# A Mamba block and a mixture of experts on one core: the skip term goes into PSUM through ScalarE, the orders of all engines are rewritten, and the last expert is finished in halves

## The chip, the cores and the metric

The kernel runs on one core of one Trainium2 chip. The metric is the device time of one execution in microseconds (us); lower is better. Before the change the median of 3 runs is 1095.29 us (1094.91 to 1095.7). The five engines of the core run their own instruction queues in order and meet at semaphores: TensorE (PE), VectorE (DVE), ScalarE (ACT), GpSimd (POOL), and SyncE (SP), which issues nearly all DMAs.

## The reference

The input holds 32 sequences of 256 tokens with 128 channels. Two residual blocks follow each other:

```python
x = x + mamba(layernorm(x))
x = x + moe(layernorm(x))

# mamba: d_inner = 256, 16 states, 4 taps, rank 8
xi, res = split(x @ W_in)
u = silu(causal_conv(xi) + conv_b)
delta_r, B, C = split(u @ W_x)
delta = softplus(delta_r @ W_dt + b_dt)
h[t] = exp(delta * A) * h[t-1] + delta * B * u        # per channel and state
y[t] = sum over states of h[t] * C[t]
y = (y + u * D) * silu(res)                           # u * D is the skip term
out = y @ W_out
# moe: 8 experts, hidden 256, the two best of them weighted by a softmax
y = sum over e of cw[:, e] * (silu(x @ w1[e].T) @ w2[e].T)
```

## The kernel before, in words

The work is cut into 16 rounds of two sequences (512 tokens). In a round a tile of the recurrence holds 128 channels by 2 halves by 512 tokens, 128x1024 elements, and there are 16 of them, one for each state n. The names of the steps are those of the functions in the code. For each state n of round j:

- PE `row_b` (L1701) spreads the row of B over the partitions into the PSUM tile `rows`; it waits until the scan of state n-2 is done, since `rows` has two places.
- DVE `inputs` (L1224) multiplies it with `du` (delta * u), and DVE `scan` (L1235) runs the recurrence into a ring of 8 tiles `h`. ACT `decay` (L847) has written exp(delta * A) into `dA`.
- POOL `outputs` (L527) multiplies `h` with the row of C.
- PE `sum_states` (L1722) adds the tile to `y_ps`, two PSUM banks, by 8 transposes: `y_ps` is the sum over the states, turned so that tokens lie on the partitions.

When all 16 states are in, ACT `copy_y` (L860) copies `y_ps` to SBUF, PE `turn_y` (L1733) transposes it back into the two banks of `work` (banks 0 and 1), and DVE `gating` (L1266) multiplies both banks with silu(res). Then come PE `project_out`, DVE `residual` and `post_stats`, POOL `inverse_deviation` (the second layernorm), ACT `post_norm`, PE `turn_x2`, ACT `copy_x2T`, PE `score`, DVE `top_two`, the routing on POOL (`gap`, `routing`) with ACT `ratio_exp` between, and for each of the 8 experts twice PE `hidden` (L1770, into PSUM), twice ACT `hidden` (the silu, L883), PE `expert` (L1779), DVE `weight_expert` (L1303) and POOL `add_expert` (L569).

The skip term u * D goes in by ACT `skip` (L837), which writes it to the SBUF tile `ud`, and PE `skip_in` (L1710), 8 transposes that open the sum in `y_ps` ahead of the 16 states.

`work` has only two PSUM banks, which all of these steps share except the recurrence (`rows` takes four, `y_ps` two). Each PE step that writes a bank has a list of former users, and `free` waits for the first of them that exists. In the last three rounds, once `rows` comes free, the table `MOVED` puts hidden layers and experts into banks 2 to 5.

The order of the work is written out by hand for each engine. `round_(i)` is the steady body (a loop over pairs of rounds); ahead of it and behind it stand lists for the first and the last rounds. Five rounds are in flight at once: a body of PE, for example, holds the recurrence of round i-2, the experts of round i-4 and the front end of rounds i and i-1.

The end of the program is the last expert of round 15: 8 matmul pairs into one bank, one DVE `weight_expert`, one POOL `add_expert`, one DMA of 256 KB.

Of the kernel before, what the change touches and what calls it, by code (L numbers as in the profile page):

```python
# [17 lines left out]
H = 2  # L18
# [23 lines left out]
TURN_X2 = ("turn_x2", 1)  # L42
SCORE = ("score", 1)
HIDDEN = ("hidden", ((0, 1), (0, 1), (1, 0), (0, 0), (1, 0), (0, 1), (0, 0), (1, 0)))
# [5 lines left out]
MOVED = {("expert", 1, 0): 5, ("expert", 1, 1): 3, ("expert", 1, 2): 2, ("expert", 1, 4): 3, ("expert", 1, 5): 2,  # L50
         ("expert", 1, 6): 3, ("expert", 1, 7): 4, ("expert", 2, 0): 1, ("expert", 2, 1): 0, ("expert", 2, 2): 3,
         ("expert", 2, 3): 5, ("expert", 2, 4): 3, ("expert", 2, 5): 2, ("expert", 2, 6): 4, ("expert", 3, 1): 0,
         ("expert", 3, 2): 0, ("expert", 3, 4): 0, ("expert", 3, 5): 0, ("expert", 3, 7): 0,
         ("hidden", 1, 0, 1): 3, ("hidden", 1, 1, 0): 4, ("hidden", 1, 1, 1): 0, ("hidden", 1, 2, 0): 2,
         ("hidden", 1, 2, 1): 1, ("hidden", 1, 3, 0): 4, ("hidden", 1, 4, 1): 4, ("hidden", 1, 5, 0): 5,
         ("hidden", 1, 6, 0): 4, ("hidden", 1, 7, 0): 5, ("hidden", 1, 7, 1): 1, ("hidden", 2, 0, 0): 1,
         ("hidden", 2, 1, 1): 2, ("hidden", 2, 2, 0): 3, ("hidden", 2, 2, 1): 4, ("hidden", 2, 3, 0): 5,
         ("hidden", 2, 3, 1): 2, ("hidden", 2, 4, 0): 4, ("hidden", 2, 4, 1): 2, ("hidden", 2, 5, 0): 1,
         ("hidden", 2, 5, 1): 4, ("hidden", 2, 6, 0): 5, ("hidden", 2, 7, 0): 3, ("hidden", 2, 7, 1): 5,
         ("hidden", 3, 2, 1): 1, ("hidden", 3, 3, 0): 1, ("hidden", 3, 3, 1): 1, ("hidden", 3, 4, 1): 1,  # L60
         ("hidden", 3, 5, 0): 1, ("project_out", 1): 0, ("project_out", 2): 0, ("score", 1): 2}
# [30 lines left out]
def mamba_moe(nc, x, W_in, conv_w, conv_b, W_x, W_dt, b_dt, A_log, D, W_out, gate_wT, w1T, w2T, out):  # L92
# [27 lines left out]
    with ExitStack() as ctx:  # L120
# [50 lines left out]
        ud = sb("ud", [P, H, T])  # L171
# [79 lines left out]
        skip_summed = sem("skip_summed")  # L251
# [26 lines left out]
        expert_added = sem("expert_added")  # L278

# [29 lines left out]

        def two_seqs(ap):  # L310
            return ap.rearrange("p (s t) -> p s t", s=SEQS)
# [8 lines left out]
        def weigh_taps(half):  # L320

            at = slice(half * P, (half + 1) * P)
            nc.vector.tensor_tensor(w_conv[:, :, at], w_in[:, at].unsqueeze(1).broadcast_to([P, TAPS, P]),
                                 taps_rows.rearrange("p (d k) -> p k d", k=TAPS)[:, :, at],
                                 ALU.mult).then_inc(w_conv_ready, 1)

        @block.sync
        def _(sp):
# [23 lines left out]
            def store_out(j):  # L352
                if not there(j):
                    return
                sp.wait_ge(expert_added, j.count(E, E))
# [19 lines left out]
            def round_(i):  # L375
                three, four, five, seven = (i.later(-k) for k in (3, 4, 5, 7))
                load_again(five)
                load_c(four, 2)
                store_c(three)
                store_out(seven)  # L380
                load_c(four, 3)
                load_c(three, 0)
                load_c(three, 1)
                load_x(i)
# [25 lines left out]
            for g in range(CGROUPS):  # L410
                load_c(lead, g)
            load_again(r[0])
            load_again(r[1])
# [4 lines left out]
            load_c(r[1], 1)  # L418
            load_x(r[5])
            load_c(r[1], 2)  # L420
# [4 lines left out]
            load_c(r[2], 2)  # L425
            load_c(r[2], 3)
            store_c(r[3])
            load_c(r[3], 0)
            load_c(r[3], 1)
            load_x(r[6])  # L430
            run(sp, round_, 7, 7, 19)
            load_again(r[14])
# [7 lines left out]
            for odd in range(2):  # L440
                sp.wait_ge(out_stored[odd], 16 * (rounds // 2))

        @block.gpsimd
        def _(pool):
# [124 lines left out]
            def add_expert(j, e):  # L569
                if not there(j):  # L570
# [6 lines left out]
            def round_(i):  # L577
                two, three, four, five = (i.later(-k) for k in (2, 3, 4, 5))
                add_soft(two)
                times_u(two)  # L580
                add_expert(five, 4)
                outputs(three, 13)
                outputs(three, 14)
                add_expert(five, 5)
                gap(four)
                outputs(three, 15)
                outputs(two, 0)
                outputs(two, 1)
                outputs(two, 2)
                add_expert(five, 6)  # L590
                routing(four)
                add_expert(five, 7)
                outputs(two, 3)
                add_expert(four, 0)
                inverse_deviation(i, 0)
                outputs(two, 4)
                outputs(two, 5)
                add_expert(four, 1)
                outputs(two, 6)
                outputs(two, 7)  # L600
                outputs(two, 8)
                outputs(two, 9)
                add_expert(four, 2)
                outputs(two, 10)
                inverse_deviation(three, 1)
                add_expert(four, 3)
                outputs(two, 11)
                outputs(two, 12)

            inverse_deviation(r[1], 0)  # L610
            inverse_deviation(r[2], 0)
# [3 lines left out]
            outputs(r[0], 3)  # L615
            outputs(r[0], 4)
# [8 lines left out]
            inverse_deviation(r[4], 0)  # L625
# [1715 lines left out]
```

## Time and profile before

| | us |
|---|---|
| median of 3 runs | 1095.29 |
| the profiled execution's own time | 1093.58 |
| its span in the trace | 1091.6 |
| PE busy | 1039.5 (95%) |
| DVE busy | 1016.8 (93%) |
| POOL busy | 961.8 (88%) |
| ACT busy | 908.1 (83%) |

The span is the stretch from the first to the last recorded instruction; 1.98 us of the execution lie around it. "Busy" is the time in which an engine had at least one instruction under way. Matmuls overlap, so the mean of one matmul in a table is longer than its step in a chain; the steps of the chain of waits are what one of them costs when PE does nothing else. A weight (the share of the span) is a mean over a start, a long steady part and an end, which have different limits, so the stretches are read apart.

### The profile page before, as it was taken

What the parts mean: (1) busy time and instruction counts of PE and PEld (TensorE: products, weight loads), DVE (VectorE), ACT (ScalarE), POOL (GpSimd) and SP (SyncE); (2) the same over time, 40 slices, a digit from 0 to 9 for tenths busy, and PEclk for the clock granted to TensorE, in tenths of its full rate; (3) what the DMA queues carried; (4) which work ended last, traced back from release to release, by engine and by line L of the source; (5) the groups of instructions that cost most, each with busy time, mean ns of one, the idle gap of its engine ahead of it and who ended that gap; (6) DMA issues with size and microseconds to landing.
All of it is one profiled execution on the core that took longest, in us unless ns stands there. A gap on an engine that the chain in (4) does not pass through costs nothing.

```text
span 1091.6 us, 18705 instructions
## 1 busy us (share of the span) xinstructions
PE 1039.5 (95%) x6150; PEld 756.5 (69%) x6150; DVE 1016.8 (93%) x1054; ACT 908.1 (83%) x1379; POOL 961.8 (88%) x891
## 2 busy tenths in 40 slices
PE   7688779999999999999999999999999999989997
PEld 4446456677777767777777777767777776767775
DVE  5999999999999999999999999999999999999721
ACT  4987877989989998998989899899989989875533
POOL 4688986999999999999999999999999999799834
PEclk9798899999999999999999999999999999989999
DMA  5331212132040313104031311303130220320000
GB/s 201 138 127 57 78 60 79 59 117 69 6 167 14 127 59 122 63 30 153 2 126 58 126 58 64 120 0 130 54 136 39 88 87 0 137 87 11 11 10 11
DMA packets 37349, 84.12 MB, mean 77 GB/s; under 512 B 3305, under 2 KB 28193, under 8 KB 28961
## 3 DMA queue, kind: packets, MB, share of 16 engines
q1 hardware_dynamic: 36864, 83.06, 21.3%
q8 instruction: 25, 0.41, 0.2%
q14 instruction: 44, 0.35, 0.1%
q10 hardware_dynamic: 416, 0.30, 0.1%
HBM read 78.63 MB, written 4.72 MB: 76 GB/s over the span
## 4 chain that ended last, share of the span: by engine, by line
PE 82%; DVE 10%; issue 4%; ACT 3%; DMA 0%; POOL 0%; POOLq 0%; DVEq 0%; ACTq 0%
PE work L1786 19%; PE work L1776 18%; PE y_ps L1728 17%; PE work L1652 9%; DVE h L1241 6%; PE rows L1707 4%; PE work L1749 2%; PE work L1636 2%; PE work L1671 2%; PE rows L1786 2%; PE work L1662 2%; DVE rows L1231 2%; PE rows L1776 1%; PE work L1697 1%; PE y_ps L1717 1%
## 5 line engine op out<-in xcount | busy, mean ns | idle before, releaser
L534 POOL TENSOR_TENSOR h<-h,c_rows 128x1024 f32<-128x1024 f32 x256 | 600.4, 2368 | 52.2 <-DVE h L1241 52.1
L1241 DVE TENSOR_TENSOR_SCAN h<-dA,rows 128x1024 f32<-128x1024 f32 x256 | 579.4, 2277 | 1.1
L855 ACT ACTIVATE dA<-delta,a_neg 128x510 f32<-128x510 f32 x512 | 326.2, 709 | 8.0 <-DVE h L1241 4.6
L1231 DVE TENSOR_TENSOR rows<-du,rows 128x1024 f32<-128x1024 f32 x256 | 306.8, 1215 | 3.9 <-PE rows L1707 3.7
L1728 PEld LDWEIGHTS y_ps<-ident,h 128*128 128x128 f32 x2048 | 241.3, 144 | 61.5 <-issue 33.5
L1728 PE MATMUL y_ps<-ident,h 128*128 128x128 f32 x2048 | 270.0, 278 | 10.7 <-POOL h L534 10.7
L1786 PEld LDWEIGHTS work<-w,hid 128*128 128x128 f32 x1856 | 223.2, 193 | 35.1 <-ACT hid L889 18.9
L1776 PE MATMUL work<-x2T,w 128*128 128x512 f32 x474 | 238.5, 598 | 3.4 <-ACT u L773 2.8
L1786 PE MATMUL work<-w,hid 128*128 128x128 f32 x1856 | 229.1, 277 | 2.7 <-ACT hid L889 2.2
L889 ACT ACTIVATE hid<-work 128x512 f32<-128x512 f32 x237 | 139.4, 596 | 64.0 <-PE work L1776 62.2
L574 POOL TENSOR_TENSOR x<-x,weighted 128x512 f32<-128x512 f32 x128 | 163.6, 1278 | 21.6 <-DVE weighted L1310 21.1
L1776 PEld LDWEIGHTS work<-x2T,w 128*128 128x128 f32 x474 | 81.7, 190 | 57.3 <-issue 19.5
L1707 PE MATMUL rows<-parts,select 96*128 96x512 bf16 x256 | 100.3, 392 | 21.1 <-DVE h L1241 19.7
L1652 PE MATMUL work<-xnT,w_conv 128*128 128x512 f32 x256 | 116.3, 597 | 0.5 <-ACT xnT L765 0.5
L739 ACT ACT_TABLE_LOAD x74 | 94.9, 1283 | 1.3
L889 ACT ACT_TABLE_LOAD x56 | 71.8, 1283 | 20.5 <-PE work L1776 14.7
L1310 DVE TENSOR_TENSOR weighted<-work,cw 128x512 f32<-128x512 f32 x116 | 78.6, 677 | 8.6 <-PE work L1786 6.8
L1652 PEld LDWEIGHTS work<-xnT,w_conv 128*128 128x128 f32 x256 | 47.4, 191 | 49.0 <-issue 47.9
L1707 PEld LDWEIGHTS rows<-parts,select 96*128 96x128 bf16 x256 | 25.4, 100 | 56.7 <-DVE h L1241 28.5
L1310 DVE TENSOR_TENSOR weighted<-rows,cw 128x512 f32<-128x512 f32 x12 | 8.2, 691 | 32.3 <-PE rows L1786 20.5
L525 POOL TENSOR_TENSOR du<-delta,u 128x1024 f32<-128x1024 f32 x15 | 35.4, 2363 | 1.8 <-POOL delta L518 1.3
L518 POOL TENSOR_TENSOR delta<-du,soft 128x1024 f32<-128x1024 f32 x15 | 35.4, 2361 | 0.0
(141 smaller groups left out, 954.3 us busy)
## 6 DMA issues: line engine op xcount, KB each, us to landing
c_rows<-c_dram SPq DMA_DIRECT2D x64, 1024.0 KB, 4.8
x_in<-in_x SPq DMA_DIRECT2D x16, 256.0 KB, 2.9
x_again<-in_x SPq DMA_DIRECT2D x16, 256.0 KB, 3.4
out<-x SPq DMA_DIRECT2D x16, 256.0 KB, 2.6
w<-in_w1T SPq DMA_DIRECT2D x1, 1024.0 KB, 4.9
w<-in_w2T SPq DMA_DIRECT2D x1, 1024.0 KB, 7.1
h<-in_conv_w SPq DMA_DIRECT2D x1, 512.0 KB, 4.8
c_dram<-bcd SPq DMA_DIRECT2D x16, 32.0 KB, 1.6
```

What stands on the lines that cost most here:

```text
L534: nc.gpsimd.tensor_tensor(at, at, c_rows[:, n, :].unsqueeze(1).broadcast_to([P, H, T]), ALU.mult).then_inc(c_used, 1)
L574: nc.gpsimd.tensor_tensor(x1[:, j.odd], x1[:, j.odd], weighted[:, e % 2], ALU.add).then_inc(expert_added, 1)
L739: nc.scalar.preload_act_table_set("natural_log_exp_and_others")
L855: last = nc.scalar.activation(two_seqs(dA[:, n % RING, half, :])[:, :, 1:], two_seqs(delta[:, half, :])[:, :, 1:], ACT.Exp, scale=a_neg[:, ...
L889: nc.scalar.activation(hid[:, e % 2, f, :], bank(place(HIDDEN, j, e, f)), ACT.Silu).then_inc(hid_ready, 1)
L1231: nc.vector.tensor_tensor(rows[:, n % 2], du[:, j.odd], rows[:, n % 2, H - 1, :].unsqueeze(1).broadcast_to([P, H, T]), ALU.mult).then_inc( ...
L1241: nc.vector.tensor_tensor_scan(h[:, n % RING].rearrange("p h t -> p (h t)"), dA[:, n % RING].rearrange("p h t -> p (h t)"), rows[:, n % 2] ...
L1652: last = nc.tensor.matmul(two_seqs(work[:, CONV[half], :]), w_conv[:, k, half * P:(half + 1) * P], xnT[:, :, k:k + SEQ], start=(k == 0), s ...
L1707: nc.tensor.matmul(rows[:, n % 2, H - 1, :], select[:, n, :], parts[:, j.odd, :], start=True, stop=True).then_inc(b_ready, 1)
L1728: last = nc.tensor.matmul(y_ps[:, half, b, :], h[:, n % RING, half, b * P:(b + 1) * P], ident[:, :], is_transpose=True, start=False, stop= ...
L1776: nc.tensor.matmul(bank(place(HIDDEN, j, e, f)), w1[:, e, f, :], x2T[:, j.odd, :], start=True, stop=True).then_inc(hid_projected, 1)
L1786: last = nc.tensor.matmul(token_bank(place(EXPERT, j, e))[:, b, :], hid[:, e % 2, f, b * P:(b + 1) * P], w2[:, f, e, :], start=(f == 0), s ...
```

## The change

- `skip` becomes one step for each half, and writes u * D straight into bank 0 or 1 of `work` (ACT, SBUF to PSUM). `turn_y` adds onto it: its transposes no longer open the bank. `skip_in`, the tile `ud` and the semaphore `skip_summed` are gone, and the first `sum_states` of a round opens `y_ps`. `skip` waits for the former users of its bank, as PE's steps do.
- The matmuls of `expert` and `project_out` open a bank once instead of once for each block of 128 tokens.
- The last expert of round 15 runs through its first hidden half for all tokens and then the second, into two banks; DVE adds cw times the expert to x1 in four 128x128 steps, without POOL, and each half is stored by a DMA of its own.
- The orders of all engines, the table of banks `HIDDEN` and `MOVED` are new. The steady body of PE starts at another step; POOL, DVE and SP issue `add_soft`, the stats of the next layernorms and the loads at other places.

```diff
-            def skip(j):
+            def skip(j, half, *uses):
                 if not there(j):
                     return
                 act.wait_ge(u_ready, j.count(H, H))
-                wait(act, skip_summed, j.count(1, 0))
-                for half in range(H):
-                    last = nc.scalar.activation(ud[:, half, :], u[:, j.odd, half, :], ACT.Copy,
-                                                scale=skip_w[:, half:half + 1])
-                last.then_inc(skip_ready, 1)
+                free(act, *uses)
+                nc.scalar.activation(bank(TURN_Y[half]), u[:, j.odd, half, :], ACT.Copy,
+                                     scale=skip_w[:, half:half + 1]).then_inc(skip_ready, 1)
...
-            def skip_in(j):
...
-                for half in range(H):
-                    for b in range(TB):
-                        last = nc.tensor.matmul(y_ps[:, half, b, :], ud[:, half, b * P:(b + 1) * P], ident[:, :],
-                                                is_transpose=True, start=(b == 0), stop=False,
-                                                skip_group_check=True)
-                last.then_inc(skip_summed, 1)
...
             def sum_states(j, n):
                 if not there(j):
                     return
                 pe.wait_ge(c_used, j.count(NS, n + 1))
+                if n == 0:
+                    wait(pe, yT_ready, j.count(1, 0))
...
-            def turn_y(j, half, *uses):
+            def turn_y(j, half):
                 if not there(j):
                     return
                 pe.wait_ge(yT_ready, j.count(1, 1))
-                free(*uses)
-                turn(work[:, TURN_Y[half], :], yT[:, half], y_turned)
+                pe.wait_ge(skip_ready, j.count(H, half + 1))
+                turn(work[:, TURN_Y[half], :], yT[:, half], y_turned, onto=True)
...
+                if is_last(j, e):
+                    pe.wait_ge(yT_ready, rounds)
+                    for f in range(FH):
+                        pe.wait_ge(hid_ready, j.count(E * FH, FH * e + f + 1))
+                        for b in range(TB):
+                            half, first = b // (TB // 2), b % (TB // 2) == 0
+                            last = nc.tensor.matmul(last_half_bank(half)[:, b, :], hid[:, e % 2, f, b * P:(b + 1) * P],
+                                                    w2[:, f, e, :], start=(first and f == 0),
+                                                    stop=(not first and f == FH - 1), skip_group_check=True)
+                            if f == FH - 1 and not first:
+                                last.then_inc((last_half_done, expert_done)[half], 1)
+                    return
...
-MOVED = {("expert", 1, 0): 5, ("expert", 1, 1): 3, ("expert", 1, 2): 2, ("expert", 1, 4): 3, ("expert", 1, 5): 2,
+MOVED = {("expert", 1, 0): 1, ("expert", 1, 1): 5, ("expert", 1, 2): 2, ("expert", 1, 3): 5, ("expert", 1, 4): 2,
...
```

The first place is on PE in the steady body, around the two `turn_y` of a round (`work<-ident,yT`). `y_ps<-ident,h` is `sum_states`, `rows<-parts,select` is `row_b`, `work<-x2T,w1` is a `hidden`, `work<-w2,hid` an `expert`. Before:

```order
L1776 MATMUL work<-x2T,w1 128x512
L1631 REGISTER_ALU
L1776 MATMUL work<-x2T,w1 128x512
L1717 MATMUL y_ps<-ident,ud 128x128 x8
L1631 REGISTER_ALU
L1636 MATMUL work<-ident,yT 128x128 x4
L1631 REGISTER_ALU
L1636 MATMUL work<-ident,yT 128x128 x4
L1728 MATMUL y_ps<-ident,h 128x128 x24
L106 REGISTER_ALU
L1707 MATMUL rows<-parts,select 128x512
L1786 MATMUL work<-w2,hid 128x128 x8
```

And now:

```order
L1874 MATMUL work<-x2T,w1 128x512
L105 REGISTER_ALU
L1814 MATMUL rows<-parts,select 128x512
L1825 MATMUL y_ps<-ident,h 128x128 x8
L1834 REGISTER_ALU
L1742 MATMUL work<-ident,yT 128x128 x8
L105 REGISTER_ALU
L1814 MATMUL rows<-parts,select 128x512
L1825 MATMUL y_ps<-ident,h 128x128 x8
L1897 MATMUL work<-w2,hid 128x128 x8
```

The 8 transposes of `ud` are gone, a `row_b` and one `sum_states` stand ahead of the turn in their place, and one `sum_states` with a `row_b` instead of three is left between the turn and the expert.

The second place is on ACT in the steady body, behind `copy_y` (`yT<-y_ps`), with the silu of two hidden halves and then the skip into `work`:

```order
L950 ACTIVATE yT<-y_ps 128x1024
L105 REGISTER_ALU
L973 REGISTER_ALU
L974 ACTIVATE hid<-work 128x512
L973 REGISTER_ALU
L974 ACTIVATE hid<-work 128x512
L929 ACTIVATE work<-u,skip_w 128x512 x2
L825 ACT_TABLE_LOAD
```

Before, the two skips stood about half a round earlier, between `copy_xnT` and the last hidden layers, and nothing on this path waited for them.

The third place is on PE at the end of the program, from the second-last `sum_states` of round 15 on. Before:

```order
L1728 MATMUL y_ps<-ident,h 128x128 x8
L1786 MATMUL work<-w2,hid 128x128 x8
L1728 MATMUL y_ps<-ident,h 128x128 x8
L1776 MATMUL rows<-x2T,w1 128x512 x2
L1636 MATMUL work<-ident,yT 128x128 x4
L1776 MATMUL rows<-x2T,w1 128x512
L1636 MATMUL work<-ident,yT 128x128 x4
L1786 MATMUL rows<-w2,hid 128x128 x8
```

And now:

```order
L1825 MATMUL y_ps<-ident,h 128x128 x16
L1874 MATMUL work<-x2T,w1 128x512
L1897 MATMUL rows<-w2,hid 128x128 x8
L1874 MATMUL rows<-x2T,w1 128x512
L1825 MATMUL y_ps<-ident,h 128x128 x8
L1897 MATMUL rows<-w2,hid 128x128 x8
L1742 MATMUL work<-ident,yT 128x128 x4
L1874 MATMUL rows<-x2T,w1 128x512
```

Before, the experts of round 14 behind the last `sum_states` begin with its third; now they begin with its fourth, and three hidden halves more stand ahead of it. From the last `sum_states` to the end PE has 27 `hidden`, 14 `expert` before and 24 and 13 now.

## Rows read from the trace of the kernel before

**Rows 1.** The page, its first part: busy time and share of the span.

```profile
PE 1039.5 (95%) x6150; PEld 756.5 (69%) x6150; DVE 1016.8 (93%) x1054; ACT 908.1 (83%) x1379; POOL 961.8 (88%) x891
```

**Rows 2.** Two stretches: length, busy PE, PEld, DVE, ACT, POOL, clock, DMA share, GB/s.

```profile
200.00:900.00 700.00, 698.02 (x4242) 514.16 (x4241) 693.05 (x718) 639.67 (x966) 665.04 (x598) 1.00 0.22 79
...
31.50:1028.60 997.10, 959.11 (x5723) 700.79 (x5724) 983.41 (x976) 869.57 (x1314) 921.90 (x807) 0.98 0.21 76
```

**Rows 3.** Groups of instructions, 200 to 900 us: busy us, mean ns, idle before.

```profile
L1241 DVE TENSOR_TENSOR_SCAN h<-dA,rows 128x1024 f32<-128x1024 f32 x178 | 403.5, 2278 | 0.8
...
L739 ACT ACT_TABLE_LOAD x56 | 71.8, 1283 | 1.0
...
L843 ACT ACTIVATE ud<-u,skip_w 128x512 f32<-128x512 f32 x22 | 14.6, 720 | 0.0
...
L1717 PE MATMUL y_ps<-ident,ud 128*128 128x128 f32 x88 | 11.4, 273 | 0.0
```

**Rows 4.** Timeline of DVE: start, length, instruction, idle time ahead of it.

```profile
99.68 1.23 DVE L1272 TENSOR_TENSOR yT<-work,gate 128x1024 f32<-128x1024 f32 x1 [1.21 <-PE work L1636]
...
133.00 2.36 DVE L1231 TENSOR_TENSOR rows<-du,rows 128x1024 f32<-128x1024 f32 x2 [2.06 <-PE rows L1707]
...
554.91 0.69 DVE L1281 TENSOR_TENSOR x<-x_again,work 128x512 f32<-128x512 f32 x1 [0.31 <-PE work L1749]
...
977.57 1.23 DVE L1231 TENSOR_TENSOR rows<-du,rows 128x1024 f32<-128x1024 f32 x1 [0.88 <-PE rows L1707]
```

**Rows 5.** Chain of waits near the end: start, length, engine, line.

```profile
991.56 0.22 PE rows L1707
991.78 0.88 PE y_ps L1728 x8
992.66 0.86 PE work L1776 x2
993.52 1.78 PE work L1786 x16
```

**Rows 6.** Timeline of ACT, PE and DVE around one steady gating.

```profile
534.52 1.03 ACT L865 ACTIVATE yT<-y_ps 128x1024 f32<-128x1024 f32 x1
...
536.28 0.60 ACT L889 ACTIVATE hid<-work 128x512 f32<-128x512 f32 x1 [0.24 <-PE work L1776]
...
536.02 1.04 PE L1717 MATMUL y_ps<-ident,ud 128*128 128x128 f32 x8
...
538.13 1.20 DVE L1272 TENSOR_TENSOR yT<-work,gate 128x1024 f32<-128x1024 f32 x1
```

**Rows 7.** Stretches of 4 us, columns as in rows 2.

```profile
228.00:232.00 4.00, 2.96 (x20) 2.45 (x20) 3.01 (x4) 3.96 (x6) 3.47 (x12) 1.00 0.00 0
...
960.00:964.00 4.00, 2.54 (x22) 2.31 (x20) 3.90 (x15) 3.99 (x7) 4.00 (x3) 1.00 0.01 2
964.00:968.00 4.00, 2.02 (x9) 1.33 (x9) 4.00 (x3) 4.00 (x7) 4.00 (x3) 0.70 0.00 2
968.00:972.00 4.00, 3.72 (x17) 3.68 (x18) 3.96 (x4) 1.59 (x5) 4.00 (x4) 0.50 0.00 0
```

**Rows 8.** Timeline of the end, all engines.

```profile
1025.11 1.21 DVE L1231 TENSOR_TENSOR rows<-du,rows 128x1024 f32<-128x1024 f32 x1
1026.35 2.29 DVE L1241 TENSOR_TENSOR_SCAN h<-dA,rows 128x1024 f32<-128x1024 f32 x1
...
1084.06 0.60 ACT L889 ACTIVATE hid<-work 128x512 f32<-128x512 f32 x1 [2.20 <-PE work L1776]
...
1084.71 2.05 PE L1786 MATMUL rows<-w,hid 128*128 128x128 f32 x16 [0.75 <-ACT hid L889]
1086.80 0.69 DVE L1310 TENSOR_TENSOR weighted<-rows,cw 128x512 f32<-128x512 f32 x1 [2.97 <-PE rows L1786]
1087.57 1.26 POOL L574 TENSOR_TENSOR x<-x,weighted 128x512 f32<-128x512 f32 x1 [2.39 <-DVE weighted L1310]
1088.86 0.37 SPq L356 DMA_DIRECT2D out<-x  x1
```

More of the change, by code:

```diff
@@ L1848, in round_ @@
-                row_b(two, 12)
-                hidden(four, 5, 0, use_expert(four, 3))
-                sum_states(two, 9)
-                hidden(four, 5, 1, use_expert(four, 4))
-                row_b(two, 13)
                 hidden(four, 6, 0, use_hid(four, 5, 0))
@@ L1868, in round_ @@
[L1868 to L1869 removed]
+                expert(four, 6, use_xnT(i), use_x2T(three), use_hid(four, 6, 1))
                 sum_states(two, 12)
[L1871 to L1873 removed]
+                sum_states(two, 13)
+                row_b(one, 1)
+                expert(four, 7, use_scores(three), use_hid(four, 7, 1))
@@ new lines, in round_ @@
+                sum_states(two, 14)
+                row_b(one, 2)
+                hidden(three, 0, 0, use_expert(four, 6), use_xnT(i), use_x2T(three))
+                hidden(three, 0, 1, use_expert(four, 7), use_scores(three))
+                sum_states(two, 15)
+                hidden(three, 1, 0, use_hid(three, 0, 0))
+                hidden(three, 1, 1, use_hid(three, 0, 1))
+                row_b(one, 3)
+                sum_states(one, 0)
+                turn_y(two, 0)
+                turn_y(two, 1)
@@ L1905, in round_ @@
[L1905 to L1915 removed]
+                         use_hid(four, 2, 0), use_u(one, 0))
@@ new lines, in round_ @@
+                row_b(one, 5)
+                convolve(i, 1, use_expert(three, 0), use_gated(two), use_hid(three, 1, 0), use_hid(three, 0, 0),
+                         use_expert(four, 6), use_xnT(i))
+                row_b(one, 6)
+                hidden(three, 2, 0, use_u(i, 0), use_gated(two), use_hid(three, 1, 1))
+                row_b(one, 7)
+                hidden(three, 2, 1, use_u(i, 1), use_expert(three, 0))
+                expert(three, 1, use_hid(three, 2, 0))
+                project_bcd(i, use_hid(three, 2, 1), use_u(i, 1))
@@ L1916, in round_ @@
+                sum_states(one, 2)
+                row_b(one, 8)
                 expert(three, 2, use_expert(three, 1))
+                take_high(i)
+                row_b(one, 9)
                 sum_states(one, 3)
-                take_high(i)
+                take_middle(i)
+                project_out(two, use_expert(three, 2), use_expert(three, 1), use_hid(three, 2, 0), use_u(i, 0),
+                            use_gated(two))
+                hidden(three, 3, 0, use_low(i), use_hid(three, 2, 1))
@@ L1919, in round_ @@
                 sum_states(one, 4)
-                row_b(one, 8)
-                take_middle(i)
+                project_gate(i, 0, use_x1(two), use_expert(three, 2), use_expert(three, 1), use_hid(three, 2, 0),
+                             use_u(i, 0))
+                row_b(one, 10)
+                delta_rank(i, 0, use_hid(three, 3, 0), use_low(i))
+                sum_states(one, 5)
+                project_gate(i, 1, use_gate(i, 0))
+                hidden(three, 3, 1, use_dt(i, 0), use_hid(three, 3, 0))
@@ L1923, in lead_in @@
+                row_b(one, 11)
+                hidden(three, 4, 0, use_gate(i, 1), use_gate(i, 0), use_x1(two), use_expert(three, 2))
+                hidden(three, 4, 1, use_hid(three, 3, 1))
+                sum_states(one, 6)
             def lead_in():
@@ L2209, in _ @@
+            turn_y(r[14], 1)
+            row_b(r[15], 4)
             expert(r[13], 0, use_gated(r[14]))
             hidden(r[13], 2, 0, use_gated(r[14]))
+            row_b(r[15], 5)
+            expert(r[13], 1, use_expert(r[13], 0))
+            sum_states(r[15], 1)
+            sum_states(r[15], 2)
+            project_out(r[14], use_expert(r[13], 1))
             row_b(r[15], 6)
-            expert(r[13], 1, use_expert(r[13], 0))
-            sum_states(r[15], 2)
+            hidden(r[13], 2, 1, use_hid(r[13], 2, 0))
```

1110 lines of the change are left out of this document (526 added, 584 removed).

## The prediction

> **What bounds the kernel now.** I read the shares first, and they don't decide it: PE 95%, DVE 93%, POOL 88% [rows 1]. So I read the steady part alone, 200 to 900 us. There PE is busy 698.0 of 700 us, DVE 693.1, POOL 665.0, ACT 639.7 [rows 2]. It holds 178 scans [rows 3], and 16 make a round, so a round takes 700 / 178 x 16 = 62.9 us; in it PE is busy 62.7 us and DVE 62.3. The reader is to see that two engines are full at once: what is taken from PE alone can shorten a round by 0.6 us at most, and less where DVE's gaps are the spacing of its own dependent instructions.
>
> The timeline of DVE shows which gaps are waits. A steady round has one, of about 0.3 us, for `project_out` ahead of `residual` [rows 4], the third row there; I count 12 rounds at that. In the first rounds DVE waits 1.21 and 2.06 us, near the end 0.88 us [rows 4], with a few smaller ones between. From the first scan to the last, DVE is busy 983.4 of 997.1 us [rows 2]: 13.7 us of gaps, of which I read some 10 as waits.
>
> Behind the last scan, which ends at 1026.35 + 2.29 = 1028.64 [rows 8], DVE has little to do. There PE alone sets the end with what is left of the experts of rounds 14 and 15, and then come one DVE, one POOL step and a store. This tail is 1091.6 - 1028.6 = 63.0 us.
>
> The sum is thus: when does the last scan end, and how long is the tail.
>
> **PE's work.** The chain of waits gives the prices while PE is full: 0.88 us for 8 transposes, 0.86 for a `hidden`, 1.78 for an `expert` [rows 5]. `skip_in` is 8 transposes, once in each of 16 rounds: 16 x 0.88 = 14 us leave PE (by its busy time, 11.4 us over 11 rounds [rows 3], it is 16.6). That is the most the change can take by this route.
>
> **The end of the last scan.** DVE's own instructions stay the same but for two small things. One `weight_expert` of round 14 now stands ahead of the last scan instead of behind it, +0.6 us. And four fewer `inputs` are followed at once by their own scan, each worth about 0.12 us (a scan right behind its own `inputs` starts 1.24 us after it [rows 8], while the second of two `inputs`, which take 2.36 together [rows 4], starts 1.12 after the first), -0.5. What can go is the waits, 10 us at most. In a steady round PE now needs 62.7 - 0.9 = 61.8 us against DVE's 62.3 to 62.6, so `project_out` is in time and 0.3 us a round should go, 3.6 in 12 rounds; of the early and late waits, some 6 us, PE's smaller load should take a good third, 2.2. Against this stands a new wait.
>
> **The new wait.** Before, `turn_y` needed only `copy_y` and free banks, and three `sum_states` (2.6 us) lay between it and the next user of bank 0, an `expert`, which waits for the gating. Now the path from the last `hidden` of the four goes: silu 0.6, skip 0.7 and 0.7 (0.72 each into SBUF [rows 3]), turn of the second half 0.44, gating. With `copy_y` at 534.5 [rows 6] ACT would be through with both silus at 536.6 and with both skips at 538.0, the turn at 538.5; before, the gating started at 538.13 with no wait [rows 6]. What queues behind a late gating on DVE is everything: the next `inputs` and the scans. DVE's new order puts the gating behind `inputs` 3 instead of behind scan 3, so it comes there 3 us earlier relative to the scans; PE, which now has slack, is earlier as well. I make it -0.7 to +0.5 us of wait a round, and take 0.15, 1.8 us in 12 rounds. PE itself will wait at the next `expert`: it has 0.22 + 0.88 us of work there [rows 5] where it had 2.9, and the gating takes 1.2, so about 1.2 us, and some 0.5 at a `row_b`. That is 1.7 us a round against a slack of 0.5 to 0.8. It still fits where PE works ahead of DVE: walked through with the prices above, the later `row_b` of the round come 0.4 to 1.6 us before DVE asks for them.
>
> The skip's price in PSUM no row shows. A 128x512 ACT copy without a scale out of PSUM is 0.60, the skip into SBUF 0.72; I bound it by 0.5 and 1.2 and take 0.7. By 1.2 the gating would be 1 us late in every round, 12 us: that is part of the slow rival. The Trainium skill ("ScalarE: Activation LUTs", step-by-step section) says that PSUM is the faster destination for ScalarE; no row here shows it, and by it the skip would fall below 0.72 and the new wait towards nothing.
>
> ACT also loads its tables less often: 8 switches a round in the new order against 10, 2 x 1.28 us [rows 3]. ACT is busy 57.5 of 62.9 us [rows 2] and DVE waits for it nowhere in the steady part, so this is worth nothing in itself; it pays for the skip being in a worse place. POOL (59.8 us busy a round) keeps its instructions. Walked through, its new order starts the steady `outputs` close behind the scans and is just in time for `sum_states`; I cost it at 0, with 0.5 a round as the bound. The DMAs are the same, and their engines are busy 22% [rows 2].
>
> So the last scan: 1028.6 + 0.6 - 0.5 - 3.6 - 2.2 + 1.8 = 1024.7.
>
> **The tail.** Behind the last `sum_states` PE has 3 `hidden` and 1 `expert` less: 3 x 0.86 + 1.78 = 4.4 us. The path behind that sum (copy, turn, gating, projection, residual, stats, deviation, norm, turn, copy) has 15.8 us of round 14's steps as cover (5 `expert`, 8 `hidden`), where it had 20.1 and PE waited for none of it. What other engines do on it is `copy_y` 1.03 and gating 1.20 [rows 6], and after the projection four short steps on DVE, POOL and ACT, together some 10 us by my estimate. So the cover holds and I take 4.3.
>
> At the very end, the last silu is done at 1084.66 and the store is issued at 1088.86, 4.2 us [rows 8]: 2.05 for the expert, 0.69 DVE, 1.26 POOL and their spacing. Now the first half of the matmuls runs before that silu, 0.9 us remain, with 0.2 of delay, then two DVE steps of 128x128 for the last half. No row has that form; 128x512 takes 0.69, so a pair lies between 0.35 and 0.9 and I take 0.6. With spacing 1.8 against 4.2: -2.4, between 1.5 and 2.7. The store's own end I leave as it is. Tail: 63.0 - 4.3 - 2.4 = 56.3.
>
> **Sum.** Span 1024.7 + 56.3 = 1081.0, 10.6 us less than 1091.6. The profiled execution took 1093.58, so 1083.0 for a like one; the median of the runs is 1.7 us above that execution, hence 1084.7. Changes within 0.2% (2.2 us) can't be told from none.
>
> **Rivals.**
>
> *PE was the only true bound (0.15).* PE's busy share of 99.7% speaks for it; DVE's 99.0% with gaps of 0.04 to 0.1 us speaks against. Then all 14 us go, and the 2.4 at the end: 1095.3 - 16.4 = 1079.
>
> *The gating eats the steady gain (0.20).* The skip makes it 0.3 to 0.5 us late in each round, as the ACT times above allow, and the early waits come back in other places. Then the last scan ends where it did, or 2 us later, and only the tail is left, 6.7 us: 1089 to 1091.
>
> *PE loses its clock in the steady part (slower, 0.09).* At 960 to 968 us PE was busy only 2.54 and 2.02 of 4 us, and behind it the granted clock fell to 0.50, half of 2.4 GHz; in 228 to 232, with 2.96 of 4, it stayed at 1.00 [rows 7]. At half clock 4 us of work need 8, so such a fall costs PE 2 to 3 us. The new order has two PE waits close together around the turn in each round, 1.7 us. If they come to 3 us, from a skip nearer to 1.2 or a late POOL, the clock falls there in every second round: 6 x (2.5 + 1.3 - 0.5) = 20 us, less 6.7: 1109. It decides against the change from about 1.1 us of net loss a round on. The Trainium skill ("TensorE: Matmul & The Clock Gate", section on psum-queue depth-cycling) says that cycling through PSUM banks can leave PE idle often and briefly enough for the clock to swing; by that rule the banks held from skip to gating would do this here. The trace agrees only in that a fall follows idle PE time; around the steady turns of the kernel before, the clock stays at 1.00.
>
> *It comes out even (0.06).* POOL half a microsecond late in each round, and a routing in the tail that comes after the experts it weights: 1093 to 1097.
>
> The forecast has 0.50, from 1081 to 1088. Faster by over 0.2%: 0.50 + 0.15 + 0.18 = 0.83; within 0.2%: 0.08; slower: 0.09. The range runs from below the first rival to the even case, 1077 to 1094.
>
> **What the new profile would show.** Right: no L1717-like transposes of `ud`; a steady round of 62.5 to 62.8 us, DVE above 99.2% busy, PE at 97%, and its idle time released by DVE's gating and scans; the last scan at 1023 to 1027; 55 to 58 us from there to the end; no POOL step behind the last expert. Wrong: DVE waiting for `work<-ident,yT` in each round (the second rival); a clock below 1.00 between 300 and 900 us (the third); DVE still above 62.8 a round with no waits at all, which would say that its work, not its waits, was underpriced; PE idle in the tail for cw or for the norm, which would say that the cover of round 14 was too thin.

## The result, and the profile of the changed kernel

The changed kernel takes 1123.81 us (median of 4 runs, 1121.13 to 1125.44) against 1095.1 for the kernel before (4 runs, 1092.95 to 1095.7). The ratio is 1.026, with a 95% interval from 1.025 to 1.028: 2.6% slower, where I had forecast 1084.7. The profiled execution took 1121.13 us, with a span of 1119.3.

The first part of the page of the changed kernel, as [rows 1]:

```profile
PE 1043.6 (93%) x6022; PEld 746.1 (67%) x6022; DVE 1018.3 (91%) x1057; ACT 889.7 (79%) x1361; POOL 960.2 (86%) x890
```

The busy times hardly differ from those of before (PE 4.1 us more, with 128 matmuls fewer; DVE 1.5 more; ACT 18 and POOL 1.6 less), and all are smaller shares of a longer span. The stretch from 200 to 900 us, with the columns of [rows 2]:

```profile
200.00:900.00 700.00, 671.71 (x3975) 485.54 (x3973) 665.70 (x681) 591.36 (x905) 637.05 (x575) 1.00 0.22 80
```

The holes in this stretch have grown: PE 28 us where it had 2, DVE 34 where it had 7, POOL 63 where it had 35. The granted clock is 1.00 over the stretch as a whole. The groups of that stretch, as [rows 3]:

```profile
L591 POOL TENSOR_TENSOR h<-h,c_rows 128x1024 f32<-128x1024 f32 x172 | 404.1, 2366 | 40.6 <-DMA c_rows<-c_dram 33.2 <-DVE h L1340 7.3
L1340 DVE TENSOR_TENSOR_SCAN h<-dA,rows 128x1024 f32<-128x1024 f32 x170 | 383.2, 2275 | 0.7
...
L929 ACT ACTIVATE work<-u,skip_w 128x512 f32<-128x512 f32 x22 | 14.2, 684 | 0.0
```

170 scans where there were 178: 700 / 170 x 16 = 65.9 us a round against 62.9. The skip into PSUM takes 684 ns, a little less than the 720 into SBUF. The new thing stands behind the first row: POOL's `outputs` waits for a DMA, `c_rows<-c_dram`, which loads the rows of C spread over the partitions. The waits in that stretch, longest first (engine, tile, line, what it waits for: us in total, times, longest), for POOL, PE and DVE:

```profile
POOL h L591 <- DMA c_rows<-c_dram: 33.2, 8, 4.6
...
PE y_ps L1825 <- POOL h L591: 23.3, 26, 1.3
...
DVE rows L1330 <- PE rows L1814: 16.3, 13, 2.5
...
DVE weighted L1422 <- POOL x L631: 9.2, 8, 1.2
```

The chain is plain: eight waits of 4.2 us, and two more at the same place (3.6 and 3.8 us, of the 7.3 that the view puts down to DVE), so ten in the ten rounds between 205 and 800 us; then PE's `sum_states` behind POOL, then DVE behind PE's `row_b`, and DVE is the engine that a round is made of. One such place on POOL (timeline, columns as in [rows 4]):

```profile
529.45 2.38 POOL L591 TENSOR_TENSOR h<-h,c_rows 128x1024 f32<-128x1024 f32 x1
535.99 7.01 POOL L591 TENSOR_TENSOR h<-h,c_rows 128x1024 f32<-128x1024 f32 x3 [4.16 <-DMA c_rows<-c_dram]
```

The DMA queue of SP around it (start, time on the sequencer, the transfer):

```profile
491.05 0.40 SPq L413 DMA_DIRECT2D out<-x  x1
526.88 0.39 SPq L390 DMA_DIRECT2D x_in<-in_x  x1
527.57 0.38 SPq L400 DMA_DIRECT2D x_again<-in_x  x1
528.06 0.44 SPq L429 DMA_DIRECT2D c_rows<-c_dram  x1
528.61 0.36 SPq L419 DMA_DIRECT2D c_dram<-bcd  x1
536.00 1.28 SPq L429 DMA_DIRECT2D c_rows<-c_dram  x3
```

`c_rows` comes in four groups of four states a round (1 MB each). The one at 528.06 is the last group of the round that POOL is in; POOL would have taken it up at 529.45 + 2.38 = 531.83. It was issued at 528.06 and landed at 535.99, 7.9 us later. It stands behind `x_in`, which SP may only issue once ACT's `pre_norm` has read the old one:

```profile
524.97 1.64 ACT L834 ACTIVATE xn<-x_in,shift,rstd 128x128 f32<-128x128 f32 x4
```

That ends at 526.61, and `x_in` goes out at 526.88. The issue ahead of it is the store of `out` at 491.05, so the queue stood for 36 us at `load_x`, and everything behind it with it. In the same place of the kernel before, the order was another:

```profile
510.60 0.39 SPq L340 DMA_DIRECT2D x_in<-in_x  x1
511.19 0.39 SPq L350 DMA_DIRECT2D x_again<-in_x  x1
512.61 0.34 SPq L372 DMA_DIRECT2D c_rows<-c_dram  x1
...
551.35 7.98 SPq L372 DMA_DIRECT2D c_rows<-c_dram  x3
```

There the `c_rows` at 512.61 is the third group, and the fourth is the first of the three from 551.35 on, ahead of the next `x_in`. In the code, the steady body of SP read `store_out(seven), load_c(four, 3), load_c(three, 0), load_c(three, 1), load_x(i)`; the changed one reads `store_out(seven), load_x(i), load_again(four), load_c(four, 3), store_c(three)`. The last load of C has been moved behind two loads of x. The page's list of DMAs shows it too, by the median time from issue to landing (KB each, us), after:

```profile
c_rows<-c_dram SPq DMA_DIRECT2D x64, 1024.0 KB, 6.7
...
c_dram<-bcd SPq DMA_DIRECT2D x16, 32.0 KB, 7.1
```

and before:

```profile
c_rows<-c_dram SPq DMA_DIRECT2D x64, 1024.0 KB, 4.8
...
c_dram<-bcd SPq DMA_DIRECT2D x16, 32.0 KB, 1.6
```

The number, size and bytes of these transfers are the same. Only what stands ahead of each is not.

Behind two of the ten waits, at 540 and 738 us, the granted clock falls too. Stretches of 4 us around the first, columns of [rows 2]:

```profile
532.00:536.00 4.00, 4.00 (x36) 3.80 (x35) 4.00 (x3) 3.59 (x5) 0.01 (x1) 1.00 0.37 139
536.00:540.00 4.00, 2.38 (x20) 1.95 (x18) 3.90 (x17) 4.00 (x8) 4.00 (x2) 1.00 0.79 272
540.00:544.00 4.00, 3.27 (x15) 3.12 (x16) 1.45 (x2) 1.82 (x5) 4.00 (x4) 0.57 1.02 428
```

POOL stands first (0.01 busy of 4), then PE (2.38), and only then is the clock at 0.57, near the lower of its two levels; DVE is hit last (1.45). The two rounds with such a fall take 67.1 and 66.9 us from gating to gating, the six others between 289 and 817 us 65.7 at the mean, so the clock makes up less than 3 us of the loss, and it comes behind POOL's wait.

### The profile page after: what moved, and what is told of

Read it like the earlier page. It is cut to its first block, busy times and chain, and to the rows that moved or that the text cites. A ratio compares the mean times of both kernels' runs of the same rounds, so it can differ in the third digit from the quotient of the medians.

```text
span 1119.3 us, 18572 instructions
## 1 busy us (share of the span) xinstructions
PE 1043.6 (93%) x6022; PEld 746.1 (67%) x6022; DVE 1018.3 (91%) x1057; ACT 889.7 (79%) x1361; POOL 960.2 (86%) x890
## 4 chain that ended last, share of the span: by engine, by line
PE 40%; DVE 26%; issue 20%; POOL 11%; ACT 2%; DVEq 1%; DMA 0%; POOLq 0%; ACTq 0%
DVE h L1340 13%; PE work L1897 8%; DVE rows L1330 8%; POOL h L591 8%; PE work L1874 8%; PE y_ps L1825 7%; PE work L1759 6%; PE rows L1897 2%; PE rows L1814 2%; POOL x L631 2%; DVE weighted L1422 2%; PE work L1742 1%; PE rows L1874 1%; PE work L1769 1%; PE work L1778 1%
## 5 line engine op out<-in xcount | busy, mean ns | idle before, releaser
L1825 PE MATMUL y_ps<-ident,h 128*128 128x128 f32 x2048 | 279.8, 282 | 32.7 <-POOL h L591 31.3
L1769 PE MATMUL work<-xnT,w_in 128*128 128x512 f32 x64 | 35.0, 630 | 0.2 <-DVE weighted L1422 0.2
```

The source lines that it names most:

```text
L1825: last = nc.tensor.matmul(y_ps[:, half, b, :], h[:, n % RING, half, b * P:(b + 1) * P], ident[:, :], is_transpose=True, start=(n == 0 and ...
```

## The experiments

The leading theory, L: the place of `load_c(four, 3)` in SP's order is the whole loss, and what is left of the change is about what I forecast. Its rivals: the skip's way through PSUM or the new orders of PE, ACT and POOL cost the time and the late DMA only shows up beside it; or the new end costs.

**1. The changed kernel with the load of C first.**

```diff
                 load_c(four, 2)
+                load_c(four, 3)
                 store_out(seven)
                 load_x(i)
                 load_again(four)
-                load_c(four, 3)
                 store_c(three)
```

and likewise, ahead of `load_x`, at two places of the list for the first rounds. The load also passes `store_out` here; as the rows above show, that store was issued 36 us before `x_in`, so it isn't what held the load.

> The changed kernel, with one edit on SP: the load of the last four C rows of a round (load_c group 3) stands ahead of store_out and of load_x, in the steady body and in the two places of the start; nothing else moves. Theory L (the loss sits in this queue: load_x waits for the pre_norm two rounds on, the C rows queue behind it, and POOL stands 4.2 us in each round until they land): POOL's waits for c_rows go from 33 us to below 3, a steady round from 66.1 to 62.5-63.0 us, and the time from 1123 to 1083-1093. Rival S (the loss is the skip that holds banks 0 and 1: turn and gating late, PE and then DVE behind it): POOL would only wait for something else, the time stays above 1112. Rival P (POOL's new order has no slack left): 1095-1110, with POOL at 95% busy and DVE waiting for row_b as now.

Measured: 1088.98 us (4 runs, 1087.64 to 1090.84); ratio to the kernel before 0.995 (0.994 to 0.997). That is 35 us below the changed kernel. The two groups that had waited:

```profile
L591 POOL TENSOR_TENSOR h<-h,c_rows 128x1024 f32<-128x1024 f32 x180 | 422.6, 2368 | 0.5 <-DVE h L1340 0.4
L1340 DVE TENSOR_TENSOR_SCAN h<-dA,rows 128x1024 f32<-128x1024 f32 x178 | 401.4, 2277 | 0.7
```

POOL's 40.6 us of idle time ahead of `outputs` are 0.5. The first half of L holds, and this kernel is faster than both, by 0.5% against the kernel before. The second half doesn't: what is left of the change is 5.4 us (1094.41 - 1088.98, the kernel before in the same set of runs), half of the 10.6 that I had forecast.

**2. The kernel before with the load of C late.** The move alone, in the old code:

```diff
                 store_out(seven)
-                load_c(four, 3)
                 load_c(three, 0)
                 load_c(three, 1)
                 load_x(i)
+                load_c(four, 3)
```

> The kernel before, with the reverse edit on SP alone: in the steady body the load of the last four C rows stands behind load_x, as in the changed kernel. Theory L: POOL's multiply of state 12 has to wait for a load that is issued only after the pre_norm two rounds on; the load would be issued about 574.3 in the round where POOL wants it about 575.6, and needs 6 to 8 us to land, so POOL stands 4 to 6 us a round; 3 to 5 us of it reach the round: 1095 to 1130-1155. Rivals S and P: the queue is innocent and the time stays within 5 us of 1095.

Measured: 1130.57 us (4 runs, 1127.09 to 1135.46), ratio 1.033 (1.030 to 1.036). Its waits, 200 to 900 us:

```profile
POOL h L534 <- DMA c_rows<-c_dram: 42.1, 9, 6.1
DVE rows L1231 <- POOL du L525: 37.6, 9, 5.6
```

The same wait, of 4.7 us at the mean, and the same size of loss, with nothing else of the change in it. It reaches DVE by another road, `du`, which stands behind the waiting `outputs` on POOL. With 1 this shows the cause from both sides. One thing differs from the changed kernel: only `x_in` stands directly ahead of the load, not both loads of x. The load is issued at 529.08, and POOL would have taken it up at 530.53, 1.5 us later; in the changed kernel POOL comes 3.8 us after the issue. So the size of the wait hangs on when `pre_norm` lets the queue go as much as on what stands ahead.

**3. The load of C between the two loads of x,** to tell which part of the path makes it late: the wait of `load_x` for `pre_norm`, or the transfer of `x_again` in front.

```diff
                 load_x(i)
-                load_again(four)
                 load_c(four, 3)
+                load_again(four)
```

> The changed kernel; on SP, in the steady body, the load of the last four C rows stays behind load_x but goes ahead of load_again, so that only the 256 KB of x_in, not both loads of x, are ahead of it. It tells how much of POOL's 4.2 us a round is the wait of the queue for pre_norm and how much is the transfers in front. Theory L: the load is issued about 0.5 us sooner after x_in (its place after load_again was 528.06, load_x 526.88) and shares the engines with 256 KB less (about 1 us): POOL's wait falls from 4.2 to 2.5-3.5 us a round, the time from 1123 to 1107-1118. If it were all wait for pre_norm, at least 1119; if all transfers, below 1100.

Measured: 1097.38 us (10 runs, 1092.96 to 1101.9), ratio 1.003 (1.002 to 1.005). I expected more, 1107 to 1118, and had set below 1100 as the sign that the transfers ahead make the whole wait: one place in the queue is worth 26 of the 35 us. The waits of POOL and DVE, 200 to 900 us:

```profile
POOL h L591 <- DMA c_rows<-c_dram: 15.4, 10, 3.7
...
DVE weighted L1422 <- POOL x L631: 2.6, 3, 1.2
```

The wait is 1.5 us a round at the mean where it was 4.1 over the ten rounds, and DVE hardly feels it: 2.6 us behind POOL's `x`. Two rounds side by side show what the place is worth. In both POOL comes 5.2 us after the end of `pre_norm`. In the changed kernel the load is issued 1.45 us after that end and lands 7.9 us later, so POOL waits 4.2; here it is issued 0.8 us after it and lands 5.4 us later, so POOL waits 1.0. Of the 3.2 us, 0.7 are the earlier issue and 2.5 the shorter landing behind `x_in` alone. Neither reason makes the wait by itself: the stop at `pre_norm` leaves only those 5.2 us, which a landing of 4.8 just fits and one behind other transfers doesn't.

POOL's slack swallows a wait of that size. The span of the profiled execution is 1091.3, 4.3 us above that of experiment 1, and counted by the scans 4.0 of it has arisen by the end of the seventh round, where the waits are 1.7 to 3.7 us; in the rounds behind, the waits are 0.6 to 1.1 us and a round takes 62.8 as in experiment 1. That execution (1093.14) is at the fast end of the ten, so the median has a larger loss that this trace doesn't show.

The Trainium skill ("DMA: Bandwidth & Descriptors", section on queues, rings and completion order) says that on each DMA engine the descriptors of one issuing engine's queue are consumed in the order of its ring. The traces agree: a 32 KB store behind 1.5 MB of loads took 7.1 us to land (median) and 1.6 before.

**4. The kernel before with the new end only** (the last expert by halves, DVE adds, two stores):

```diff
+                    for f in range(FH):
+                        pe.wait_ge(hid_ready, j.count(E * FH, FH * e + f + 1))
+                        for b in range(TB):
+                            half, first = b // (TB // 2), b % (TB // 2) == 0
+                            last = nc.tensor.matmul(last_half_bank(half)[:, b, :], hid[:, e % 2, f, b * P:(b + 1) * P],
```

> The kernel before with the new end alone: the last expert by halves into two banks, four 128x128 steps on DVE that add it to x1, no POOL step, two stores. By the prediction's sum -2.4 us (1.5 to 2.7), so 1092.4 to 1093.8. If the two DVE steps of a half cost more than 0.9 us, or the second store takes as long as the whole one did and adds its own start, the gain is below 1 us.

Measured: 1091.27 us (8 runs, 1090.24 to 1093.01), ratio 0.997 (0.996 to 0.998), 3.1 us less where I had expected 2.4. From the end of the last silu to the store:

```profile
1084.43 0.60 ACT L904 ACTIVATE hid<-work 128x512 f32<-128x512 f32 x1 [2.20 <-PE work L1804]
...
1085.91 0.61 DVE L1330 SCALAR_TENSOR_TENSOR x<-rows,cw,x 128x128 f32<-128x128 f32 x2 [1.71 <-PE rows L1819]
1086.44 0.60 DVE L1330 SCALAR_TENSOR_TENSOR x<-y_ps,cw,x 128x128 f32<-128x128 f32 x2
```

The silu is done at 1085.03, DVE at 1087.04: 2.0 us, where silu to store was 4.2 [rows 8]. A pair of the new DVE steps takes 0.60, as taken. From the end of the last silu to the end of the span it is 4.4 us here and 6.9 in the kernel before, 2.6 less.

**5. The kernel before without `skip_in`.** The skip term is left out of the sum; ACT still computes it. This gives the most that taking 8 transposes from PE can bring in the old order.

```diff
-                skip_in(one)
...
-                                                ident[:, :], is_transpose=True, start=False, stop=(n == NS - 1),
+                                                ident[:, :], is_transpose=True, start=(n == 0 and b == 0), stop=(n == NS - 1),
```

> The kernel before without skip_in: the skip term is left out of the sum (ScalarE still makes it, nobody reads it), and the first sum_states opens the bank. Orders untouched, so PE loses 0.88 us in each of 16 rounds and nothing else changes. It tells what PE's relief is worth by itself. If DVE's own work bounds the round (a_c3_first stands at 62.77 us a round with hardly a wait, before at 62.98), a round goes from 62.98 to 62.65-62.8 and the kernel gains 2 to 5 us: 1090-1093. If PE was the bound, it gains 12 to 14 us: 1080-1083.

Measured: 1090.1 us (4 runs, 1088.93 to 1091.62), ratio 0.996 (0.994 to 0.997), 3.7 us less. So of 16 x 0.88 = 14 us of PE work, 3.7 are felt. DVE's timeline has two gatings, six rounds apart:

```profile
410.99 1.20 DVE L1271 TENSOR_TENSOR yT<-work,gate 128x1024 f32<-128x1024 f32 x1
...
787.57 1.20 DVE L1271 TENSOR_TENSOR yT<-work,gate 128x1024 f32<-128x1024 f32 x1
```

376.58 / 6 = 62.76 us a round. And of experiment 1:

```profile
409.38 1.23 DVE L1371 TENSOR_TENSOR yT<-work,gate 128x1024 f32<-128x1024 f32 x1
...
786.02 1.23 DVE L1371 TENSOR_TENSOR yT<-work,gate 128x1024 f32<-128x1024 f32 x1
```

376.64 / 6 = 62.77. A round with the skip in PSUM is as short as one with no skip at all, against 62.98 in the kernel before, whose gatings start at 412.16 and 790.03, 377.87 / 6. So in the steady rounds the gain is whole, and small: DVE sets it. That is the steady part alone, and the two kernels differ in all their orders; the last scan of this one starts at 1023.25, 2.1 us ahead of that of experiment 1.

**6. Experiment 1 with the skip undone:** ACT writes `ud` again and PE's `skip_in` adds it, in the new orders. ACT's `skip` moves too, from behind the silus to ahead of the first `decay` of the round.

```diff
-            def skip(j, half, *uses):
+            def skip(j):
...
+            def skip_in(j):
+                pe.wait_ge(skip_ready, j.count(1, 1))
```

> The changed kernel with the same SP edit as a_c3_first, and the skip undone: ScalarE writes u*D to SBUF ahead of the first decay of the round, PE opens y_ps with 8 transposes of it ahead of the first sum_states, turn_y opens its banks and waits for their former users; the orders are otherwise those of the change. Against a_c3_first: if the skip through PSUM takes 0.88 us of PE a round and costs a gating wait of some 0.3 us, a_c3_first is 0 to 6 us faster; rival S says that this kernel is the faster one, by 5 us or more; if DVE alone bounds the round, the two are within 3 us.

Measured: 1129.27 us (4 runs, 1128.02 to 1131.12), ratio 1.033 (1.031 to 1.034), 40 us above experiment 1. A clear miss. Its gatings:

```profile
413.39 1.23 DVE L1360 TENSOR_TENSOR yT<-work,gate 128x1024 f32<-128x1024 f32 x1 [1.39 <-PE work L1731]
482.96 1.23 DVE L1360 TENSOR_TENSOR yT<-work,gate 128x1024 f32<-128x1024 f32 x1 [1.39 <-PE work L1731]
547.15 1.23 DVE L1360 TENSOR_TENSOR yT<-work,gate 128x1024 f32<-128x1024 f32 x1 [1.39 <-PE work L1731]
```

Rounds of 69.6 and 64.2 us take turns. The 64.2 is 62.8 plus the wait of 1.39 in each round. Two things now stand on the path to `turn_y`: `skip_in`, 0.87 us, and ACT, which with its `skip` at the earlier place brings two silus 1.2 us later against the scans, so that PE waits for it:

```profile
PE work L1873 <- ACT hid L977: 9.7, 12, 0.9
```

The 5.4 us more in every second round look like this on PE:

```profile
580.15 0.60 PE L1793 MATMUL work<-parts,w_dt 96*128 96x512 bf16 x2 [1.85 <-issue]
580.59 0.61 PE L1896 MATMUL work<-w,hid 128*128 128x128 f32 x4
583.10 2.72 PE L1896 MATMUL work<-w,hid 128*128 128x128 f32 x12 [1.90 <-issue]
```

"issue" is time in which PE waited for nothing that the profile shows, once in the middle of an `expert`, whose 16 matmuls need nothing new after the fourth. The granted clock falls behind it to 0.75 and 0.50, and DVE waits 4.95 us for a `row_b`. The body of the loop holds two rounds, so both stops come once in each pass. The page's list of queues has a row that goes with it, here:

```profile
q8 instruction: 61, 1.00, 0.4%
```

(packets, MB, share). The packets are 25 in the kernel before, 24 in experiments 1 and 5, and 61 here. The trace has their times, too. In experiment 1 there is none between 422 and 946 us, while PE goes round its loop (until 941), and in the kernel before none between 411 and 935. Here nine of 16 KB come in each pass of the loop, and in the pass that begins at 576.3 the first three start at 577.3, 580.6 and 584.4, around the two stops (578.3 to 580.1 and 581.2 to 583.1). So here the loop is loaded anew in each pass, and in the others it isn't. That PE waits in the two stops for its instructions is still an inference, from these times, the place and the period; the profile names no releaser.

**7. The same with two waits fewer in PE's loop,** to see whether the loop was one or two instructions too long for something.

```diff
-                pe.wait_ge(yT_ready, j.count(1, 1))
+                if half == 0:
+                    pe.wait_ge(yT_ready, j.count(1, 1))
```

> a_c3_pe_skip (1129.3) with two wait instructions fewer in PE's loop: turn_y of the second half doesn't repeat its wait for copy_y. In a_c3_pe_skip every second round took 69.6 us against 64.2: PE stood twice 1.9 us with nothing that it waited for, the granted clock fell behind it, and the page counts 61 packets of instruction loads on a queue that has 24 or 25 in all other kernels; PE's loop has one instruction more than that of the kernel before. Theory I (PE's loop is just too long to be kept, and part of it is fetched anew in each pass): 24-25 packets, all rounds 64.2 us, 1098-1108 in all, and against a_c3_first (1089) that is what the skip on PE costs in this order, through a gating 1.4 us late. Rival: the stall is a wait that the profile doesn't show, for a bank or for ACT, and the time stays at 1124-1132.

Measured: 1125.36 us (4 runs, 1122.43 to 1128.22), ratio 1.027 (1.025 to 1.029). The packets are still 61 and both stops are there. I had expected 1098 to 1108 if the loop was too long. The waits turned out to ride on instructions that remain: a pass of the loop has 1,643 records on PE in both traces, so this says nothing on length. The kernel before has 1,637 in a pass and no such stop, the changed kernel 1,613. A limit between 1,637 and 1,643 isn't ruled out, and where the loop lies wasn't varied. This stays open. It also means that experiment 6 doesn't price the skip's move; 5 beside 1 does so for the steady rounds alone.

## Why the prediction was wrong, step by step

**The step that failed: "The DMAs are the same, and their engines are busy 22%".** With it went POOL's "I cost it at 0, with 0.5 a round as the bound". The DMAs are the same in number and bytes; their order in SP's queue is not, and a mean share of 22% says nothing on when one transfer lands. I read PE, ACT, POOL and DVE place by place and never SP. The price could have been worked out: the diff moves `load_c(four, 3)` behind `load_x`, whose issue waits for `pre_norm`, so its time is the start of `pre_norm` plus its length plus two issues plus a landing of at least 4.8 us behind 512 KB, against the fourth group's use on POOL. Measured, it lands 4.2 us late in each round. About 1 us of that POOL absorbs and 3.2 remain (66.0 us a round, from gatings at 420.26 and 684.39 four rounds apart, against 62.77). With ten such rounds that makes the 32 us by which the last scan is later than in experiment 1 (1057.64 against 1025.36):

```profile
1057.64 2.27 DVE L1340 TENSOR_TENSOR_SCAN h<-dA,rows 128x1024 f32<-128x1024 f32 x1
```

```profile
1025.36 2.27 DVE L1340 TENSOR_TENSOR_SCAN h<-dA,rows 128x1024 f32<-128x1024 f32 x1
```

(the changed kernel, then experiment 1). Behind it both take the same: 1119.3 - 1059.9 = 59.4 and 1087.0 - 1027.6 = 59.4. So of the error of 39 us, 35 are this step (1123.8 - 1089.0), and 4 come from the terms below, which experiment 1 lets me read one by one. (On the spans they are 6.0, 1087.0 against 1081.0; I had added 1.7 to come from one execution to the median, which that kernel doesn't need.)

**The last scan: forecast 1024.7, in experiment 1 1027.6, 1.0 us earlier than before.** The steady waits: 3.6 less 1.8 for the new gating wait, so 1.8 net; measured 62.98 - 62.77 = 0.21 a round, 2.5 in 12, so the net was nearly right. Its two terms weren't: the waits for `project_out` are 1.9 us in all in the kernel before, not 3.6, and the steady gating doesn't wait. That they nearly cancel was luck. DVE's remaining waits in 200 to 900 us of experiment 1:

```profile
DVE yT L1371 <- PE work L1742: 1.6, 2, 0.8
DVE rows L1330 <- PE rows L1814: 1.2, 2, 0.8
```

The gating waits twice in eleven rounds, both times ahead of 284 us, and not in each. What failed was "PE's smaller load should take a good third" of the early and late waits, -2.2: with -2.5 in the steady part and +0.1 for DVE's own work, -1.0 in all leaves +1.4 there. From the first scan to the last DVE waits 9.5 us in the kernel before, 1.9 of them for `project_out` in the steady rounds, and 8.6 in experiment 1, where none of that kind is left: so 7.6 us of other waits became 8.6. In the first two rounds they did shrink, and the scans are 2.8 us ahead at the end of the second; in the next three they come back, with 2.2 for `row_b` and two gatings 0.8 late, and 1.1 of the lead is lost. The last round gives back 3.0 more, nearly all of it DVE's own work that the new order puts there (a second `top_two`, another `weight_expert` and an `inputs`). A share of a third for waits that I hadn't followed one by one was a guess.

**The tail: forecast 56.3, measured 59.4.** "Behind the last `sum_states` PE has 4.4 us less" is true, but that work stands ahead of it now, and PE was behind DVE already. The last `sum_states` of experiment 1:

```profile
1033.23 1.04 PE L1825 MATMUL y_ps<-ident,h 128*128 128x128 f32 x8
```

With its 0.88 it ends near 1034.1, 6.5 us behind the last scan. In the kernel before:

```profile
1031.90 1.04 PE L1728 MATMUL y_ps<-ident,h 128*128 128x128 f32 x8
```

ends near 1032.8, 4.1 us behind that kernel's last scan at 1028.64. So 2.3 of the 4.4 us that I took off the tail came back as a later sum, which I had tied to the scan as if PE could keep up. From the end of that sum to the end of the last silu it is 51.9 us before and 48.6 here, 3.3 less where I had 4.4; what holds the other 1.1 I haven't traced. The new end was forecast at -2.4 and brings 2.6 in the traces of experiments 1 and 4 (3.1 by the medians of experiment 4, with the spread of the runs in it). So 63.0 + 2.3 - 3.3 - 2.6 = 59.4.

**The skip.** Bounds 0.5 to 1.2, taken 0.7, measured 0.684. The Trainium skill ("ScalarE: Activation LUTs", step-by-step section) says that PSUM is the faster destination for ScalarE; here it is by 5%, 684 ns against 720. PE waits 0.2 us a round for it, and 0.3 for the gating at the next `expert` where I had put 1.2:

```profile
PE work L1897 <- DVE yT L1371: 3.5, 11, 0.3
...
PE work L1742 <- ACT work L929: 2.2, 11, 0.3
```

**The rivals.** None was the cause. "PE was the only bound" is refuted by experiment 5 (3.7 us of 14). "The gating eats the steady gain" is refuted by the two waits in eleven rounds. But with the load of C put right, experiment 1 measures 1089.0, at the edge of that rival's 1089 to 1091 and outside my 1081 to 1088: the steady gain came, and what ate it were the other waits, the late sum and DVE's last round. The clock rival (slower, 0.09) came nearest on the side and in its last link: the clock does fall in the steady part, twice. But its price and place were for a gating or skip that comes late, neither of which does; the fall follows POOL's wait for a DMA and goes with it. "POOL half a microsecond late in each round" had the right engine, with an eighth of the size and no DMA in it. No rival had a transfer in it, so the range of 1077 to 1094 left the true case out.

## What to carry to other kernels

Read the diff of the queue that issues the DMAs as closely as that of the engines: for each load that moved, take the last thing that the loads ahead of it wait for, add their issues and its landing time, and compare that with when its reader comes to it. A mean DMA share doesn't bound this, and a landing time in the table holds only for what stood ahead in that trace. Where work is moved from behind a step to ahead of it, ask first whether the engine is waiting there; if it is behind, the step itself moves by that much.

## What the runs showed of the hardware that I had not expected

- One 256 KB load ahead in the same queue was worth 2.5 us of POOL's wait in each round (experiment 3 beside the changed kernel: 15.4 us in ten waits against 40.6), the issue 0.6 us earlier included; and the last group of C took 7.9 us to land behind two of them, where the median was 4.8.
- A loop of 1,637 PE records ran its passes without one packet in the instruction queue, and one of 1,643 drew nine of 16 KB in each pass (experiments 6 and 7). With them PE stopped twice a pass for 1.4 to 2.1 us, once in the middle of a run of matmuls, which cost 5.4 us a pass in experiment 6. What brings the loading on is open.
- Taking 14 us from an engine that is busy 99.7% of the steady part gave 3.7, since a second one was full as well.
